# Moving the low halves of the x blocks from VectorE to GpSimd, each ahead of the tap products two steps later

## The chip, the cores and the metric

The kernel runs on one core of a Trainium2 chip. The metric is the time of one execution on the device in microseconds (us); less is better. The core has TensorE (PE, matmuls; its weight loads are listed apart as PEld), VectorE (DVE), ScalarE (ACT), GpSimd (POOL) and the queue engine SyncE (SP), which only issues transfers here.

## The reference, cut to what matters

```python
# x: (4, 512, 16, 32), float32
x = x + conv_mix(ln_c(x), w3, w7, w15, w_mix)      # causal depthwise convs of 3, 7, 15 taps, then a 96 -> 32 mix
t = to_tokens(x)                                    # 2048 tokens of 512
t = t + moe(ln_t(t), gate_w, w1, w2, w3)            # 8 experts, top 2: (silu(t w1) * (t w3)) w2
```

## The kernel before, in words

Every float32 product is made on TensorE as three products of a high and a low half: a = hi + lo, where hi is the value rounded to the type that TensorE takes at full rate (float32r) and lo = a - hi. So each tile that TensorE reads needs two further instructions: a copy that makes hi (ScalarE), and a subtraction that makes lo.

The program has three stages. The first is the convolution, written as matmuls: for each output block, the filter taps times the mixing matrix (the "tap products", a 128 x 512 to 128 x 1280 matrix `wc`) are the weights, and a normalised block of x, shifted, is what streams. The second routes the tokens, the third runs the experts. The change touches the first alone.

The first stage runs in 26 steps t. Steps 0 to 14 are five output blocks of three steps each (4, 4 and 6 tiles of 128 columns of `wc`, so 512, 512 and 768 columns); steps 15 to 25 are one output block each. While steps 0 to 14 run, the 16 blocks of x are still being prepared, one a step. There is no scheduler: each engine's list is written out by hand, and semaphores (counters that one engine raises and another waits for) tie them together. For step t these instructions are what the text below speaks of:

- DVE, iteration t: `x_join(t+1)` (four BATCH_NORM_AGGREGATE from PSUM, L1117), `x_stats(t+2)` (four BATCH_NORM_STATS2, L1108, and `spread`, a TENSOR_TENSOR of 96 elements, L1111), `x_scales(t+1)` (RECIPROCAL, L1122, and `nb`, a SCALAR_TENSOR_TENSOR of 4 elements, L1123), `wc_low(t)` (the low half of the tap products, L1149), `x_low(t)` (the low half of block t of x, L1143), and after steps 2, 5, 8, 11 `add_conv` (L1154), which takes a finished output block out of PSUM.
- ACT, iteration t: `x_deviation(t+1)` (a square root, L597), `x_normal(t+1)` (four ACTIVATE that write the normalised block `xs`, L604, and one that writes its high half, L609), `wc_high(t+2)` (L592).
- POOL: `multiply_taps(t)`, the tap products of step t (L442, in one to four instructions), which waits for `wc_low(t-3)`, since `wc` has three buffers. For t from 3 on these are POOL's only work in this stage.
- PE, iteration t: `x_moments(t+2)` (L791; x_join needs its result, and it needs `spread`), then `conv(t)` (L823 to L825), which waits for `x_low(t)` and `wc_low(t)`.
- SP: `join_halves`, transfers that copy parts of two finished x blocks side by side for the last product of an output block. They wait for `x_low` of those blocks.

`xs` has two buffers, so `x_normal(t+1)` also waits for `x_low(t-1)`.

Of the kernel before, what the change touches and what calls it, by code (L numbers as in the profile page):

```python
# [8 lines left out]
ALU = mybir.AluOpType  # L9
# [8 lines left out]
NBLK = 16  # L18
# [4 lines left out]
PAD = max(LAGS) // NQ - 1  # L23
WB = 3
# [49 lines left out]
def ended(t):  # L74
    return [p for p in range(NBLK) if last_step(p) == t]
# [20 lines left out]
def chunks(t):  # L96

    h = NBLK - 1 - (t // NS if t < NS * LONG else t - 2 * LONG)
    two = pair(h)
    single = [p for p in head_parts(h) if p not in two]  # L100
    each = two + tuple(single)
    runs = [(n, blk, j, LAGS[n] // NQ - (1 if (n, blk, j) in two else 0)) for n, blk, j in each]
    if t < NS * LONG:
        runs = [runs[t % NS]]
    if t >= NS * LONG or t % NS == NS - 1:
        runs.append((two[0][0], None, 1 if two[0][2] == 1 else 0, 1))
    return runs
# [24 lines left out]
def metaformer(nc, xt, taps_d, mix_d, joint_d, gate_d, units, out):  # L132

    with ExitStack() as ctx:
        def at(name, byte, shape, dt=F32):

            with ExitStack() as s:
                if byte:
                    s.enter_context(nc.sbuf_tensor(f"under_{name}", [P, byte // 4], F32))
                return s.enter_context(nc.sbuf_tensor(name, shape, dt))  # L140

        def sem(name):
            return ctx.enter_context(nc.semaphore(name))
# [7 lines left out]
        xs_hi, xs_lo = xs_parts[:, :, 0, :, :], xs_parts[:, :, 1, :, :]  # L151
# [5 lines left out]
        xs = [at(f"xs{n}", small_at + 2944 + 2 * KB * n, [P, NB, P]) for n in range(2)]  # L157
# [103 lines left out]
        pads = sem("pads")  # L261
        x_spread, x_hop, x_var, x_sd, x_scale = (sem("x_spread"), sem("x_hop"), sem("x_var"), sem("x_sd"),
                                                 sem("x_scale"))
        x_norm, x_hi_out, x_lo_out = sem("x_norm"), sem("x_hi_out"), sem("x_lo_out")
# [64 lines left out]
        def _(sp):  # L329
# [12 lines left out]
            def join_halves(p):  # L342

                blocks = [NBLK - 1 - blk for _, blk, _ in pair(NBLK - 1 - p)]
                last = LAGS[pair(NBLK - 1 - p)[0][0]] // NQ - 1
                sp.wait_ge(x_lo_out, max(blocks) + 1)
                if p >= ZB:
                    sp.wait_ge(step_ps, last_step(p - ZB) + 1)
                for m, r in enumerate(blocks):
                    for half in range(2):  # L350
                        rows = slice(2 * D * m + D * half, 2 * D * m + D * half + D)
                        sp.dma_start(joint[p % ZB][rows].bitcast(F32),
                                     xs_parts[2 + half::NQ, r, :, :, PAD - last:PAD - last + P].bitcast(F32)
                                     ).then_inc(joint_st[p % ZB], 16)
# [51 lines left out]
        def _(pool):  # L406
# [22 lines left out]
            def multiply_taps(t):  # L429

                if t >= WB:
                    pool.wait_ge(wc_lo_out, t - WB + 1)
                at_col = 0
                head = NBLK - 1 - (t // NS if t < NS * LONG else t - 2 * LONG)
                for n, blk, j, count in chunks(t):
                    first, shape = TAP_AT[n] + LAGS[n] * (blk or 0), [P, count, D, NQ]
                    lags, mixing = taps[:, first:first + count * NQ], mixT[:, j, :]
                    if blk is None:
                        pool.wait_ge(joint_in, 16)
                        lags = joint_w[:, NQ * head:NQ * head + NQ]  # L440
                        mixing = joint_w[:, NBLK * NQ + D * j:NBLK * NQ + D * j + D]
                    ins = pool.tensor_tensor(  # L442
                        wc[t % WB][:, at_col:at_col + count * P].rearrange("p (a d q) -> p a d q", d=D, q=NQ),
                        lags.rearrange("p (a q) -> p a q", q=NQ).unsqueeze(2).broadcast_to(shape),
                        mixing.unsqueeze(1).unsqueeze(3).broadcast_to(shape), ALU.mult)
                    at_col += count * P
                ins.then_inc(wc_ready, 1)
# [21 lines left out]
            pool.iota(tokid[:], pattern=[[P, NT]], base=1, channel_multiplier=1, **flat).then_inc(consts, 1)  # L469

            pool.wait_ge(taps_in[1], 16)
            for t in range(WB, STEPS):
                multiply_taps(t)

            def gather(buffer, index, landed):
# [310 lines left out]
        def _(pe):  # L786
# [14 lines left out]
            def conv(t, between):  # L801

                pe.wait_ge(x_lo_out, min(t + 1, NBLK))
                pe.wait_ge(wc_lo_out, t + 1)
                p = t // NS if t < NS * LONG else t - 2 * LONG
                opens, closes = t >= NS * LONG or t % NS == 0, last_step(p) == t
                if opens and p >= 2:
                    pe.wait_ge(resid, p - 1)
                out_bank = B[p % 2][:].rearrange("p (b i) -> p b i", i=P)
                at_col = 0  # L810
                runs = chunks(t)
                for m, (n, blk, _, count) in enumerate(runs):
                    if m == 1 and t >= NS * LONG:
                        between()
                    if blk is None:
                        pe.wait_ge(joint_st[p % ZB], 64 * (p // ZB + 1))
                    for a in range(count):
                        cols, at_x = slice(at_col, at_col + P), slice(PAD - a, PAD - a + P)
                        hi, lo = ((joint[p % ZB][:, 0, :, :], joint[p % ZB][:, 1, :, :]) if blk is None else
                                  (xs_hi[:, NBLK - 1 - blk, :, at_x], xs_lo[:, NBLK - 1 - blk, :, at_x]))  # L820
                        first = opens and m == 0 and a == 0
                        final = closes and m == len(runs) - 1 and a == count - 1
                        pe.matmul(out_bank, wc_hi[t % WB][:, cols], hi, start=first, stop=False)  # L823
                        pe.matmul(out_bank, wc_hi[t % WB][:, cols], lo, start=False, stop=False)  # L824
                        ins = pe.matmul(out_bank, wc_lo[t % WB][:, cols], hi, start=False, stop=final)  # L825
                        at_col += P
                ins.then_inc(step_ps, 1)
# [268 lines left out]
        def _(dve):  # L1096
# [29 lines left out]
            def x_stats(r):  # L1126
                dve.wait_ge(x_in[r], 16)
                if r >= 2:
                    dve.wait_ge(x_hop, r - 1)
                spread_moments(XT[r], r % 2).then_inc(x_spread, 1)  # L1130

            def x_join(r):
                dve.wait_ge(x_hop, r + 1)
                join_moments(6 + r % 2, 4 + r % 2).then_inc(x_var, 1)

            def x_scales(r):
                dve.wait_ge(x_sd, r + 1)
                scale_of(4 + r % 2).then_inc(x_scale, 1)

            def x_low(r):  # L1140
                dve.wait_ge(x_hi_out, r + 1)
                dve.wait_ge(pads, 2)
                dve.tensor_tensor(xs_lo[:, r, :, PAD:], xs[r % 2][:], xs_hi[:, r, :, PAD:], ALU.subtract).then_inc(x_lo_out, 1)  # L1143

            def wc_low(t):

                cols = slice(0, columns(t))
                dve.wait_ge(wc_hi_out, t + 1)
                dve.tensor_tensor(wc_lo[t % WB][:, cols], wc[t % WB][:, cols], wc_hi[t % WB][:, cols],  # L1149
                                  ALU.subtract).then_inc(wc_lo_out, 1)  # L1150

            def add_conv(p):
                dve.wait_ge(step_ps, last_step(p) + 1)
                ins = dve.tensor_tensor(XT[p][:], B[p % 2][:].rearrange("p (b i) -> p b i", i=P), XT[p][:], ALU.add)  # L1154
                ins.then_inc(resid, 1)
# [94 lines left out]
            for t in range(NS * LONG):  # L1250
                x_join(t + 1)
                if t + 2 < NBLK:
                    x_stats(t + 2)
                x_scales(t + 1)
                wc_low(t)
                x_low(t)
                for p in ended(t - 2):
                    if p < LONG - 1:
                        add_conv(p)
            x_low(NBLK - 1)  # L1260
            wc_low(NS * LONG)
            dve.wait_ge(consts, CONSTS)
            then_next(dve.tensor_tensor(upto_e[:], rank8[:].unsqueeze(1).broadcast_to([P, E, E]),
# [208 lines left out]
```

## Time and profile before

| | us |
|---|---|
| median of 3 runs | 774.92 (774.66 to 775.23) |
| profiled execution, its own time | 776.01 |
| its span, first to last instruction | 774.3 |
| PE busy | 725.0 (94%) |
| DVE busy | 353.6 (46%) |
| ACT busy | 321.2 (41%) |
| POOL busy | 198.2 (26%) |

The profile is one execution, recorded by the hardware. The shares are means over three stages with different limits: PE is 94% busy overall, and its pauses sit at the start, in the stretch up to 76 us, and around the routing at 147 to 200 us. So the first stage has to be read by itself, from its own rows.

### The profile page before, as it was taken

How to read it: one execution, taken by the hardware profiler on the slowest of the kernel's cores; microseconds unless marked ns; L12 is line 12 of the kernel's file. 1: busy time of each engine (PE TensorE's matmuls, PEld its weight loads, DVE VectorE, ACT ScalarE, POOL GpSimd, SP SyncE). 2: the span in 40 equal slices, each digit the busy share in tenths (PEclk: the TensorE clock that was granted, in tenths of full speed). 3: DMA queues.
4: the chain of work that ended last, by engine and by line, in shares of the span. 5: the costliest groups of instructions: out<-in, count | busy, mean ns of one | idle time of the engine just before them, and what ended most of it. 6: DMA issues, size and time to landing. Idle time of an engine off the chain costs nothing.

```text
span 774.3 us, 9557 instructions
## 1 busy us (share of the span) xinstructions
PE 725.0 (94%) x3544; PEld 588.5 (76%) x3545; DVE 353.6 (46%) x749; ACT 321.2 (41%) x504; POOL 198.2 (26%) x208
## 2 busy tenths in 40 slices
PE   3998999855999999999999999999999999999994
PEld 2776888743778778877888887778888888888883
DVE  5887756785336225531543452245325334532410
ACT  6777555543135415333434442344435234443310
POOL 5337311003601240124011502510252224021011
PEclk9999999955999999999999999999999999999998
DMA  7336777662243653074318414721653274152013
GB/s 243 66 60 112 149 169 157 158 233 68 70 193 125 188 139 113 14 217 110 112 29 257 113 55 105 236 72 54 201 126 113 41 245 122 59 151 28 3 14 42
DMA packets 55970, 92.20 MB, mean 119 GB/s; under 512 B 7536, under 2 KB 40688, under 8 KB 49776
## 3 DMA queue, kind: packets, MB, share of 16 engines
q1 hardware_dynamic: 45728, 71.64, 30.3%
q0 software_dynamic: 9472, 19.43, 12.8%
q8 instruction: 32, 0.52, 0.3%
q10 hardware_dynamic: 720, 0.46, 0.2%
q14 instruction: 18, 0.15, 0.1%
HBM read 65.49 MB, written 17.63 MB: 107 GB/s over the span
## 4 chain that ended last, share of the span: by engine, by line
PE 85%; DVE 7%; DMA 2%; issue 2%; ACT 2%; POOL 1%; SPq 0%; POOLq 0%; ACTq 0%; DVEq 0%
PE bank L920 22%; PE bank L922 22%; PE bank L921 22%; PE bank L823 3%; PE bank L824 3%; PE bank L825 3%; PE bank L915 2%; PE bank L990 2%; PE bank L845 1%; DVE bn L1108 1%; DVE wc_lo L1149 1%; PE bank L1012 1%; PE bank L863 1%; DVE mv L1117 1%; PE bank L838 1%
## 5 line engine op out<-in xcount | busy, mean ns | idle before, releaser
L920 PE MATMUL bank<-xT_hi,w_hi 128*128 128x512 f32 x495 | 194.1, 392 | 1.5 <-DVE xT_lo L1323 1.5
L922 PE MATMUL bank<-xT_hi,w_lo 128*128 128x512 f32 x495 | 193.8, 392 | 0.0
L921 PE MATMUL bank<-xT_lo,w_hi 128*128 128x512 f32 x495 | 193.8, 392 | 0.0
L496 POOL DMA_INDIRECT out_x<-y,dst_i x40 | 62.1, 1553 | 265.1 <-ACT y L690 130.4
L1330 DVE TENSOR_TENSOR h<-bank,h 128x512 f32<-128x512 f32 x64 | 44.2, 691 | 175.9 <-PE bank L922 175.9
L321 DVE TENSOR_TENSOR w_lo<-w_raw,w_hi 128x2048 fp32r<-128x2048 f32 x48 | 109.7, 2288 | 17.6 <-ACT w_hi L316 17.5
L920 PEld LDWEIGHTS bank<-xT_hi,w_hi 128*128 128x128 f32 x495 | 93.6, 189 | 21.4 <-DVE xT_lo L1323 1.8
L922 PEld LDWEIGHTS bank<-xT_hi,w_lo 128*128 128x128 f32 x495 | 93.5, 189 | 19.6
L921 PEld LDWEIGHTS bank<-xT_lo,w_hi 128*128 128x128 f32 x495 | 93.6, 189 | 19.5
L920 PE MATMUL bank<-w_hi,hT_hi 128*128 128x512 f32 x249 | 99.2, 398 | 0.0
L922 PE MATMUL bank<-w_hi,hT_lo 128*128 128x512 f32 x249 | 97.3, 391 | 0.0
L921 PE MATMUL bank<-w_lo,hT_hi 128*128 128x512 f32 x249 | 97.0, 389 | 0.0
L316 ACT ACTIVATE w_hi<-w_raw 128x2048 fp32r<-128x2048 f32 x48 | 91.8, 1912 | 7.0 <-DMA w_raw<-in_units 7.0
L675 ACT ACTIVATE hT_hi<-h 128x512 fp32r<-128x512 f32 x64 | 40.4, 632 | 120.3 <-DVE h L1330 120.3
L477 POOL DMA_INDIRECT xg<-xn_rows,src_i x32 | 33.2, 1039 | 203.3 <-PE bank L915 143.8
L669 ACT ACTIVATE h<-bank 128x512 f32<-128x512 f32 x64 | 38.3, 598 | 110.0 <-PE bank L922 110.0
L690 ACT ACTIVATE y<-bank,gate_row 128x512 f32<-128x512 f32 x32 | 22.0, 688 | 126.9 <-PE bank L922 126.9
L1323 DVE TENSOR_TENSOR xT_lo<-bank,xT_hi 128x512 fp32r<-128x512 f32 x32 | 22.1, 690 | 95.3 <-ACT xT_hi L661 95.3
L1334 DVE TENSOR_TENSOR hT_lo<-h,hT_hi 128x512 fp32r<-128x512 f32 x64 | 44.4, 693 | 44.6 <-ACT hT_hi L675 44.6
L823 PE MATMUL bank<-xs_parts,wc_hi 128*128 128x512 f32 x128 | 54.9, 429 | 6.5 <-DVE xs_parts L1143 6.5
L442 POOL TENSOR_TENSOR wc<-taps,mixT 128x256 f32<-128x256 f32 (+4 forms) x48 | 41.7, 887 | 74.1 <-DVE wc_lo L1149 71.4
L922 PEld LDWEIGHTS bank<-w_hi,hT_lo 128*128 128x128 f32 x249 | 46.7, 188 | 10.2
(166 smaller groups left out, 885.7 us busy)
## 6 DMA issues: line engine op xcount, KB each, us to landing
w_raw<-in_units SPq DMA_DIRECT2D x48, 1024.0 KB, 5.2
joint<-xs_parts SPq DMA_DIRECT2D x64, 128.0 KB, 3.8
out_x<-XT SPq DMA_DIRECT2D x17, 256.0 KB, 3.5
XT<-in_x SPq DMA_DIRECT2D x16, 256.0 KB, 6.8
xn_rows<-xnb SPq DMA_DIRECT2D x16, 256.0 KB, 2.5
gate_row<-gate_rows,gate_i POOLq DMA_INDIRECT x40, 2.8
out_x<-y,dst_i POOLq DMA_INDIRECT x40, 4.8
xg<-xn_rows,src_i POOLq DMA_INDIRECT x32, 4.0
```

The source lines that it names most:

```text
L316: eng.activation(w_hi[k][:], raw[:], ACT.Copy).then_inc(hi_ready[k], 1)
L321: eng.tensor_tensor(w_lo[k][:], raw_of(e, k)[0][:], w_hi[k][:], ALU.subtract).then_inc(lo_ready[k], 1)
L442: ins = pool.tensor_tensor(wc[t % WB][:, at_col:at_col + count * P].rearrange("p (a d q) -> p a d q", d=D, q=NQ), lags.rearrange("p (a q) ...
L496: pool.indirect_dma_start(out=out, out_offset=bass.IndirectOffsetOnAxis(ap=index, axis=0), in_=rows, in_offset=None, compute_op=ALU.add).t ...
L669: act.activation(h[m % 2][:], B[2 * (m % 2)][:], ACT.Silu).then_inc(silu_out, 1)
L675: act.activation(hT_hi[:, m, :], h[m % 2][:], ACT.Copy).then_inc(hT_hi_out, 1)
L823: pe.matmul(out_bank, wc_hi[t % WB][:, cols], hi, start=first, stop=False)
L920: pe.matmul(bank, stationary[0], moving[0], start=start, stop=False)
L921: pe.matmul(bank, stationary[0], moving[1], start=False, stop=False)
L922: return pe.matmul(bank, stationary[1], moving[0], start=False, stop=stop)
L1330: dve.tensor_tensor(h[m % 2][:], B[2 * (m % 2) + 1][:], h[m % 2][:], ALU.mult).then_inc(h_out, 1)
L1334: dve.tensor_tensor(hT_lo[:, m, :], h[m % 2][:], hT_hi[:, m, :], ALU.subtract).then_inc(hT_lo_out, 1)
```

## The change

`x_low` goes from DVE's list to POOL's. It computes the same subtraction from the same tiles into the same place. On POOL, `x_low(0)` stands ahead of the loop over the tap products, and `x_low(t-2)` ahead of `multiply_taps(t)` for t = 3 to 17. The `pads` wait falls away, since POOL writes the pads itself.

```diff
@@ gpsimd
             pool.wait_ge(taps_in[1], 16)
+
+            def x_low(r):
+                pool.wait_ge(x_hi_out, r + 1)
+                pool.tensor_tensor(xs_lo[:, r, :, PAD:], xs[r % 2][:], xs_hi[:, r, :, PAD:], ALU.subtract).then_inc(x_lo_out, 1)
+
+            x_low(0)
             for t in range(WB, STEPS):
+                if t - WB + 1 < NBLK:
+                    x_low(t - WB + 1)
                 multiply_taps(t)
@@ vector
-            def x_low(r):
-                dve.wait_ge(x_hi_out, r + 1)
-                dve.wait_ge(pads, 2)
-                dve.tensor_tensor(xs_lo[:, r, :, PAD:], xs[r % 2][:], xs_hi[:, r, :, PAD:], ALU.subtract).then_inc(x_lo_out, 1)
-
@@
                 wc_low(t)
-                x_low(t)
                 for p in ended(t - 2):
                     if p < LONG - 1:
                         add_conv(p)
-            x_low(NBLK - 1)
             wc_low(NS * LONG)
```

Where it stands on the engines: first POOL, before, from the end of its constants (`tokid`) into the loop, steps 3 to 5 and on. `wc` is the tap products, `wc_lo_out` the count of finished `wc_low`.

```order
29 L469 IOTA tokid 128x16
30 L442 TENSOR_TENSOR wc<-taps,mixT 128x512 [waits wc_lo_out,taps_in1]
31 L442 TENSOR_TENSOR wc<-taps,mixT 128x512 [waits wc_lo_out]
32 L442 TENSOR_TENSOR wc<-taps,mixT 128x640 [waits wc_lo_out]
33 L442 TENSOR_TENSOR wc<-joint_w 128x128 [waits joint_in]
```

POOL at the same place after the change; L475 is `x_low`, and `x_hi_out` counts the high halves that ACT has written.

```order
29 L469 IOTA tokid 128x16
30 L475 TENSOR_TENSOR xs_parts<-xs,xs_parts 128x4x128 [waits x_hi_out,taps_in1]
31 L475 TENSOR_TENSOR xs_parts<-xs,xs_parts 128x4x128 [waits x_hi_out]
32 L442 TENSOR_TENSOR wc<-taps,mixT 128x512 [waits wc_lo_out]
33 L475 TENSOR_TENSOR xs_parts<-xs,xs_parts 128x4x128 [waits x_hi_out]
34 L442 TENSOR_TENSOR wc<-taps,mixT 128x512 [waits wc_lo_out]
35 L475 TENSOR_TENSOR xs_parts<-xs,xs_parts 128x4x128 [waits x_hi_out]
36 L442 TENSOR_TENSOR wc<-taps,mixT 128x640 [waits wc_lo_out]
37 L442 TENSOR_TENSOR wc<-joint_w 128x128 [waits joint_in]
```

The tap products of a step now also stand behind ACT's high half of a block of x, and a subtraction and a product follow each other.

DVE before, its iteration for step 2 (768 columns), and the first instruction of the next.

```order
37 L1111 TENSOR_TENSOR spread<-bn_0,maskq 128x96 [waits dve_step]
38 L1122 RECIPROCAL rs<-rs 128x4 [waits x_sd]
39 L1123 SCALAR_TENSOR_TENSOR nb<-mv,rs 128x4 [waits dve_step]
40 L1149 TENSOR_TENSOR wc_lo<-wc,wc_hi 128x768 [waits wc_hi_out]
41 L1143 TENSOR_TENSOR xs_parts<-xs,xs_parts 128x4x128 [waits pads,x_hi_out]
42 L1117 BN_AGGR mv<-bank 128x2 [waits x_hop]
```

DVE after, the same place; the lines of the file have moved, the instructions are the same ones.

```order
35 L1119 TENSOR_TENSOR spread<-bn_0,maskq 128x96 [waits dve_step]
36 L1130 RECIPROCAL rs<-rs 128x4 [waits x_sd]
37 L1131 SCALAR_TENSOR_TENSOR nb<-mv,rs 128x4 [waits dve_step]
38 L1152 TENSOR_TENSOR wc_lo<-wc,wc_hi 128x768 [waits wc_hi_out]
39 L1125 BN_AGGR mv<-bank 128x2 [waits x_hop]
```

One instruction has gone from each iteration, the one between `wc_low` and the next `x_join`.

## Rows read from the trace of the kernel before

**Rows 1.** Windows: busy us (instructions) of each engine, granted clock, DMA share, GB/s
```profile
14.00:76.00 62.00, 57.64 (x238) 45.35 (x239) 49.52 (x187) 46.78 (x103) 30.17 (x30) 1.00 0.41 76
76.00:147.00 71.00, 71.00 (x401) 60.59 (x401) 49.90 (x206) 38.28 (x88) 14.35 (x31) 1.00 0.79 166
```

**Rows 2.** Waits from 12 to 80 us: engine, releaser, total us, times, longest
```profile
PE bank L823 <- DVE xs_parts L1143: 6.5, 10, 2.3
```

**Rows 3.** Timeline of DVE, steps 7 and 8: start, us, instruction, [idle before]
```profile
40.01 0.63 DVE L1117 BATCH_NORM_AGGREGATE mv<-bank 128x2 f32<-128x24 f32 x4 [1.55 <-PE bank L791]
40.56 0.81 DVE L1108 BATCH_NORM_STATS2 bn<-XT 128x6 f32<-128x128 f32 x4
41.41 0.26 DVE L1111 TENSOR_TENSOR spread<-bn,maskq 128x96 f32<-128x96 f32 x1
...
41.79 0.16 DVE L1123 SCALAR_TENSOR_TENSOR nb<-mv,rs 128x4 f32<-128x4 f32 x1
...
42.47 0.68 DVE L1143 TENSOR_TENSOR xs_parts<-xs,xs_parts 128x512 fp32r<-128x512 f32 x1
43.07 0.68 DVE L1154 TENSOR_TENSOR XT<-bank,XT 128x512 f32<-128x512 f32 x1
...
45.52 0.95 DVE L1149 TENSOR_TENSOR wc_lo<-wc,wc_hi 128x768 fp32r<-128x768 f32 x1
46.38 0.69 DVE L1143 TENSOR_TENSOR xs_parts<-xs,xs_parts 128x512 fp32r<-128x512 f32 x1
...
51.88 0.63 DVE L1117 BATCH_NORM_AGGREGATE mv<-bank 128x2 f32<-128x24 f32 x4 [1.61 <-PE bank L791]
```

**Rows 4.** Timeline of PE: the first matmuls of steps 8 and 14
```profile
47.13 0.51 PE L823 MATMUL bank<-xs_parts,wc_hi 128*128 128x512 f32 x1 [0.62 <-DVE xs_parts L1143]
...
71.25 0.50 PE L823 MATMUL bank<-xs_parts,wc_hi 128*128 128x512 f32 x1 [1.26 <-DVE xs_parts L1143]
```

**Rows 5.** Timeline, all engines: high half of block 0 and the start of step 0
```profile
11.10 0.63 ACT L609 ACTIVATE xs_parts<-xs 128x512 fp32r<-128x512 f32 x1
...
12.77 0.69 DVE L1149 TENSOR_TENSOR wc_lo<-wc,wc_hi 128x512 fp32r<-128x512 f32 x1
...
13.37 0.68 DVE L1143 TENSOR_TENSOR xs_parts<-xs,xs_parts 128x512 fp32r<-128x512 f32 x1
...
14.11 0.79 PE L823 MATMUL bank<-xs_parts,wc_hi 128*128 128x512 f32 x1 [2.30 <-DVE xs_parts L1143]
```

**Rows 6.** Timeline of POOL: an affine select and two tap products
```profile
1.83 0.52 POOL L423 TENSOR_SCALAR_AFFINE_SELECT sumq<-ones 128x128 f32<-128x128 f32 x1
...
5.60 1.05 POOL L442 TENSOR_TENSOR wc<-taps,mixT 128x512 f32<-128x512 f32 x1 [2.66 <-DMA mixT<-in_mix]
...
24.49 0.40 POOL L442 TENSOR_TENSOR wc<-joint_w 128x128 f32<-128x128 f32 x1
```

**Rows 7.** Timeline, all engines: POOL and DVE where both have work
```profile
72.11 0.69 DVE L1143 TENSOR_TENSOR xs_parts<-xs,xs_parts 128x512 fp32r<-128x512 f32 x1 [0.91 <-ACT xs_parts L609]
...
72.21 1.28 POOL L442 TENSOR_TENSOR wc<-taps,mixT 128x384 f32<-128x384 f32 x1
...
72.72 2.12 DVE L1149 TENSOR_TENSOR wc_lo<-wc,wc_hi 128x1280 fp32r<-128x1280 f32 x1
...
73.45 1.64 POOL L442 TENSOR_TENSOR wc<-joint_w 128x128 f32<-128x128 f32 x1
```

**Rows 8.** Timeline, all engines: two small DVE instructions beside tap products
```profile
7.11 2.26 POOL L442 TENSOR_TENSOR wc<-taps,mixT 128x512 f32<-128x512 f32 x2
...
9.16 0.23 DVE L1123 SCALAR_TENSOR_TENSOR nb<-mv,rs 128x4 f32<-128x4 f32 x1
...
24.71 0.29 DVE L1111 TENSOR_TENSOR spread<-bn,maskq 128x96 f32<-128x96 f32 x1
```

**Rows 9.** Timeline of ACT: block 8 of x, normalised, and its high half
```profile
41.98 1.65 ACT L604 ACTIVATE xs<-XT,nb,rs 128x128 f32<-128x128 f32 x4 [1.00 <-DVE nb L1123]
43.67 0.63 ACT L609 ACTIVATE xs_parts<-xs 128x512 fp32r<-128x512 f32 x1
```

## The prediction

> **What bounds the kernel now.** I read the windows first, since the shares of the whole span mix three stages. From 76 to 147 us PE is busy for 71.00 us of 71.00 [rows 1]: whatever PE gains or loses before 76 us is passed on unchanged. From 14 to 76 us, the steps 0 to 14 that the change touches, it is busy for 57.64 of 62.00 us, so at most 4.4 us lie there, and a little before 14 us. The granted clock is full (1.00) in both windows, with pauses such as the 1.26 us before 71.25 [rows 4] in them, so I charge nothing for the clock. The table of waits says what PE waits for: ten times, 6.5 us in all, for the low half of x [rows 2], 2.3 us of it ahead of its first matmul [rows 5]; 4.2 us are left for the other nine.
>
> The timeline of DVE shows why [rows 3]. In every three steps there is one stretch in which DVE works without a gap from the join of the moments at 40.01 to the low half at 46.38, through two iterations and an `add_conv`; 0.06 us after the end of that low half PE starts step 8 at 47.13 [rows 4]. The next such stretch begins at 51.88, when PE is through step 8 and the next moments. So the loop is 7.12 us on DVE and 4.75 us on PE, 11.87 us for three steps. Two `x_low` lie in the first part.
>
> **What the change removes.** An `x_low` occupies DVE for 0.60 us (from 42.47 to 43.07) [rows 3]. The first of the two leaves the loop with 0.60; the second leaves it with 0.61, because PE then waits for `wc_low` (0.95 from 45.52, so 46.47) and not for 46.38 + 0.69 = 47.07. That is 1.21 us off each three steps. At the start, step 0 waits for `wc_low` (12.77 + 0.69 = 13.46) in place of 14.05 [rows 5]: 0.6 us off. `x_low(0)` on POOL does not stand in the way: its input is there at 11.73 [rows 5].
>
> **What it costs on POOL.** The trace of before shows no GpSimd subtraction of two full tiles. The nearest row is the tap product of the same 512 elements, 1.05 us with nothing beside it; the other end is an affine select, 0.52 us for 128 elements, 2.1 us for 512 [rows 6]. The product has two inputs and one output like the subtraction, but its inputs are repeated small ones, so I take 1.10 us, near that row, and keep 1.05 and 2.1 as ends. POOL has the time: per step 1.10 and 1.05 (or 1.27 + 0.40 for the six-tile steps, 1.27 being 1.05 and another 128 elements by the slope of (1.05 - 0.40)/3 = 0.22) in about 4 us, and the low half is ready well before PE asks for it.
>
> **What it costs on DVE: turns at the memory.** This decides the sign. At 72.11 DVE reads two tiles of SBUF. POOL's product of 384 elements, which begins at 72.21, would take 0.84 by the slope and takes 1.28: it ends at 73.49 as if it had begun at 72.65, when DVE had read its 512 elements. DVE's next subtraction, of 1280 elements from 72.72, would take 1.49 (0.69 for 512 and 0.95 for 768 make 0.26 for each 256 more) and takes 2.12: it is held until 73.35, 0.14 before POOL's end. And POOL's product of 128 elements, 0.40 alone, then takes 1.64 [rows 7]: it had to let the waiting DVE go first. So an instruction of one of the two that reads two SBUF tiles excludes such a one of the other for its whole length, and who waits gets the next turn. DVE's small ones obey it too: `nb` took 0.23 for 0.16 at 9.16, until 0.14 before the end (9.37) of two tap products, and `spread` 0.29 for 0.26 at 24.71, until 0.14 before the end (24.89) of one [rows 8]. Instructions with one SBUF input (the moments, the reciprocal, `add_conv`) are not held: `add_conv` at 43.07 took its 0.68 beside a tap product [rows 3].
>
> The Trainium skill has this as a rule ("SBUF — State Buffer", Who interferes with whom): a DVE instruction with two SBUF inputs contends with a GpSimd instruction that reads SBUF, and the later one blocks fully; the trace agrees, with the 2.12 us. Its page "GPSIMD Engine Reference" (3.1) has 4497 ns for a two-input add of 2048 elements, so an estimate of 1.1 to 1.2 us for ours; the sum below would be the same within 0.4 us.
>
> Before the change POOL reads for one product a step, set off by the end of `wc_low`, while DVE goes on to `x_low` and then to the moments: hardly ever is DVE the one that waits. Now `x_low(t)` and `multiply_taps(t+2)` stand back to back, 2.1 us, set off by ACT's high half. I walk the loop with this, 0 being the join at 40.01, POOL's lock lasting until 0.14 before its end:
>
> - `x_low(7)` starts at about 0.2, 0.05 after ACT's high half of block 7, and `multiply_taps(9)` behind it holds the memory from 1.2 to 2.1. `spread` arrives at 1.4 and waits until 2.1: **0.75 lost**.
> - `nb` goes out at 2.5, and 0.2 later ACT starts block 8: 1.69 to its high half, and 0.63 for it [rows 9]. So `x_low(8)` starts at 5.1. DVE meanwhile does `wc_low(7)`, `add_conv`, the next moments (join 0.55, statistics 0.85) and comes to `spread` at 5.2: it waits until 6.06, **0.86 lost**.
> - `multiply_taps(10)` is at the memory until 7.1; `nb` comes at 6.45: **0.65 lost**. Then `wc_low(8)`, and PE starts step 8 at 8.2 where it was 7.12.
>
> The third iteration loses next to nothing: DVE waits there for ACT or PE anyway. So 2.26 lost against 1.21 won: +1.05 us for three steps.
>
> **The sum.** Start: -0.5 (0.6, less a little for `wc_low(0)` waiting for POOL). Three full loops, steps 2 to 11: +3.2. The last, steps 11 to 14: the four pieces of `multiply_taps(15)` are short, DVE gets in after some 0.3 and 0.2, and step 14 now waits for `wc_low(14)`; of the 1.05 I leave 0.4. Together +3.1 us, and PE is full afterwards, so this is the kernel's. On the profiled execution, 776.01 us (span 774.3), it makes 779.1; that one ran 1.1 us above the median of 774.92, to which the same sum gives **778.0**. With 1.05 or 1.2 us for `x_low` the same walk gives +2.4 to +3.5. SP's transfers of the joined halves wait for `x_low` of two blocks and are used at the end of a step, several us later; they hide.
>
> **The rivals.** The measurement tells 0.2% (1.55 us) from no change.
>
> 1. *The turns cost DVE little, and the kernel is faster.* If `spread` and `nb` slip in between POOL's two instructions, or POOL's requests come a little later than I have them, the 1.21 per loop is won. PE then keeps only the part of its waits that ACT sets, about 0.5 of the 1.26 before step 14: -0.6 at the start and -3.5 of the 4.2, so -4.1 us, 771. It decides where less than 1.2 us per loop is lost. For it: the two locks on `nb` and `spread` seen so far cost 0.07 and 0.03, so their full length is my extension from the 1280-element row. Against it: their ends agree with the same 0.14.
> 2. *Only part is lost*, say `spread` or `nb` and not both: about 1.2 against 1.2, 774 to 776, no difference.
> 3. *GpSimd's subtraction is much slower*, as a select is. Each 0.1 us more is met by `spread` in nearly every step, 0.25 us a loop and 1.2 over five loops. At 1.5 us this is +6, at 2.1 us about +15: 781 to 790. For it: another output type (fp32r) than any GpSimd row writes; against: the product's row.
> 4. *The subtraction on POOL delays the tap products* and through `wc_high` the next step. It has 3.5 us from one high half to the next and needs 2.2 to 2.8, so this alone costs nothing at 1.10, and joins rival 3 above 1.7 us.
>
> **How the numbers follow.** My forecast 0.52 (776.5 to 780.5 by itself), rival 1 0.22, rival 2 0.12, rival 3 with 4 0.14. Faster by over 0.2%: 0.22; same 0.13, with a little of the forecast's lower edge; slower 0.65. The range takes in rival 1 and the lower half of rival 3: 770.5 to 784.
>
> **What would show it.** In the new trace: `x_low` on POOL at 1.1 us when alone; `spread` and `nb` with durations of 0.8 to 1.1 us instead of 0.26 and 0.16, two or three times in three steps; PE's waits ascribed to `wc_low`, some 1.4 us before steps 5, 8 and 11, in place of 0.62; from 76 us on nothing changed but the shift. Step 0 starts near 13.6. I am wrong if `spread` keeps its 0.26 beside POOL's work (rival 1), or if `x_low` shows 1.5 us or more outside any overlap (rival 3).

## The result, and the profile after

The changed kernel takes **782.3 us** (median of 5 runs, 781.28 to 783.01) against 774.92 (774.06 to 775.85) of the kernel before: a ratio of 1.0089, 95% interval 1.0078 to 1.0100. It is slower, by 7.4 us where 3.1 were forecast. Timed a second time, on another occasion, it took 781.2 us (4 runs, 780.3 to 782.63) against 775.1: 1.0077, 1.0060 to 1.0094. The two profiled executions are closer together than the medians, 781.28 against 776.01 us (spans 779.3 and 774.3), since that of before lay 1.1 us above its median and that of after 1.0 below. The accounts below are of these two.

The head of the page of after, busy time of each engine and its share of the span:

```profile
PE 725.2 (93%) x3544; PEld 588.2 (75%) x3545; DVE 355.0 (46%) x733; ACT 320.4 (41%) x504; POOL 220.3 (28%) x224
```

The windows of after, the counterpart of [rows 1], with the columns named there; the windows of 2 us lie around step 14:

```profile
14.00:76.00 62.00, 52.79 (x220) 40.85 (x221) 48.13 (x166) 44.80 (x101) 41.09 (x38) 0.99 0.40 71
74.00:76.00 2.00, 0.62 (x2) 0.56 (x3) 2.00 (x2) 1.97 (x5) 2.00 (x3) 0.82 1.23 218
76.00:78.00 2.00, 2.00 (x6) 1.62 (x5) 1.97 (x3) 0.71 (x2) 2.00 (x2) 0.50 1.20 158
78.00:80.00 2.00, 2.00 (x8) 1.56 (x7) 0.81 (x2) 0.62 (x1) 2.00 (x4) 0.83 1.18 233
81.00:152.00 71.00, 71.00 (x403) 60.80 (x402) 49.56 (x204) 38.33 (x88) 15.32 (x33) 1.00 0.72 154
```

From 14 to 76 us PE is busy for 52.79 us instead of 57.64, and POOL for 41.09 instead of 30.17. DVE has 21 instructions fewer in that window but only 1.39 us less busy time (48.13 against 49.52): what it saved in subtractions it spends inside other instructions. After 81 us PE is full again at a full clock, so the loss is made before; only some 0.8 us of it comes back later. And from 76 to 78 us the granted clock is 0.50, half, which has no counterpart in the kernel before.

The table of waits of after, 12 to 85 us, and POOL and DVE in the groups of the first 80 us (count, busy us, mean ns, idle before):

```profile
PE bank L831 <- DVE wc_lo L1152: 11.0, 9, 2.2
```

```profile
L475 POOL TENSOR_TENSOR xs_parts<-xs,xs_parts 128x512 fp32r<-128x512 f32 x16 | 20.6, 1288 | 22.3 <-ACT xs_parts L617 22.3
L1131 DVE SCALAR_TENSOR_TENSOR nb<-mv,rs 128x4 f32<-128x4 f32 x16 | 8.8, 551 | 0.5
L1119 DVE TENSOR_TENSOR spread<-bn,maskq 128x96 f32<-128x96 f32 x16 | 8.6, 536 | 0.5
```

PE's waits for the low half of x [rows 2] are gone, and 11.0 us of waits for `wc_low` stand in their place. GpSimd's subtraction takes 1.29 us each of 16 times. `nb`, which works on 4 elements a partition, takes 551 ns on average and `spread` 536.

One loop of three steps of after, from the timeline of all engines (the counterpart of [rows 3]):

```profile
40.25 0.63 ACT L617 ACTIVATE xs_parts<-xs 128x512 fp32r<-128x512 f32 x1
...
40.48 0.63 DVE L1125 BATCH_NORM_AGGREGATE mv<-bank 128x2 f32<-128x24 f32 x4 [1.35 <-PE bank L799]
...
40.96 1.29 POOL L475 TENSOR_TENSOR xs_parts<-xs,xs_parts 128x512 fp32r<-128x512 f32 x1 [0.35 <-ACT xs_parts L617]
...
41.87 0.50 DVE L1119 TENSOR_TENSOR spread<-bn,maskq 128x96 f32<-128x96 f32 x1
...
42.21 1.07 POOL L442 TENSOR_TENSOR wc<-taps,mixT 128x512 f32<-128x512 f32 x1
...
42.49 0.81 DVE L1131 SCALAR_TENSOR_TENSOR nb<-mv,rs 128x4 f32<-128x4 f32 x1
...
43.82 0.68 DVE L1157 TENSOR_TENSOR XT<-bank,XT 128x512 f32<-128x512 f32 x1
44.05 0.47 PE L831 MATMUL bank<-xs_parts,wc_hi 128*128 128x512 f32 x1 [0.55 <-DVE wc_lo L1152]
...
45.72 1.29 POOL L475 TENSOR_TENSOR xs_parts<-xs,xs_parts 128x512 fp32r<-128x512 f32 x1 [2.44 <-ACT xs_parts L617]
45.80 1.32 DVE L1119 TENSOR_TENSOR spread<-bn,maskq 128x96 f32<-128x96 f32 x1
...
46.96 1.07 POOL L442 TENSOR_TENSOR wc<-taps,mixT 128x512 f32<-128x512 f32 x1
47.24 0.80 DVE L1131 SCALAR_TENSOR_TENSOR nb<-mv,rs 128x4 f32<-128x4 f32 x1
...
47.97 0.95 DVE L1152 TENSOR_TENSOR wc_lo<-wc,wc_hi 128x768 fp32r<-128x768 f32 x1
...
49.06 0.47 PE L831 MATMUL bank<-xs_parts,wc_hi 128*128 128x512 f32 x1 [1.42 <-DVE wc_lo L1152]
```

Read each DVE row beside the POOL row above it. `spread` of 45.80 goes out 0.08 us after GpSimd's subtraction (45.72 to 47.01) and ends at 47.12; `nb` of 47.24 ends at 48.04, with the product (46.96 to 48.03). `add_conv` at 43.82, which has one input in PSUM, took its 0.68. Against the 0.26 and 0.16 of [rows 3] the two lose 0.24, 0.65, 1.06 and 0.64: 2.59 us in this loop, against 1.21 won by the subtractions removed. Their ends follow from the 0.14 us that the prediction read off [rows 8]: 47.01 - 0.14 + 0.26 is 47.13 for `spread`, 48.03 - 0.14 + 0.16 is 48.05 for `nb`. The loop is 13.29 us long (joins at 40.48 and 53.77) instead of 11.87: 8.58 on DVE, until 49.06, and 4.71 on PE. By PE's waits it comes to nearly the same: 1.42 us in place of 0.62 before the third step of the loop, and a new wait of 0.55 before its second (44.05), 1.35 more in all.

The starts of steps by PE's timeline, before and after:

| step | before | after | difference | gained since the row above |
|---|---|---|---|---|
| 0 | 14.11 | 13.81 | -0.30 | -0.30 |
| 2 | 23.46 | 22.57 | -0.89 | -0.59 |
| 11 | 58.99 | 62.31 | +3.32 | +4.21 |
| 14 | 71.25 | 75.38 | +4.13 | +0.81 |
| 15 | 75.35 | 81.19 | +5.84 | +1.71 |

The last row is the clock. PE's timeline of after, around step 14:

```profile
75.38 0.77 PE L831 MATMUL bank<-xs_parts,wc_hi 128*128 128x512 f32 x1 [2.21 <-DVE wc_lo L1152]
...
76.80 0.63 PE L831 MATMUL bank<-xs_parts,wc_hi 128*128 128x512 f32 x1
...
78.83 0.40 PE L833 MATMUL bank<-xs_parts,wc_lo 128*128 128x512 f32 x1
...
81.19 0.40 PE L831 MATMUL bank<-xs_parts,wc_hi 128*128 128x512 f32 x1
```

PE waits for 2.21 us, then works through some three microseconds in which one matmul takes 0.63 us and not 0.40; the granted clock there is 0.50, which is the lower of the two levels, 1.2 GHz instead of 2.4. Step 14 is 5.81 us long instead of 4.10.

What ends that wait stands in the same stretch of the timeline of all engines:

```profile
71.99 1.29 POOL L475 TENSOR_TENSOR xs_parts<-xs,xs_parts 128x512 fp32r<-128x512 f32 x1
72.06 1.27 ACT L600 ACTIVATE wc_hi<-wc 128x1280 fp32r<-128x1280 f32 x1 [0.34 <-POOL wc L442]
...
73.23 0.28 ACT L605 ACTIVATE rs<-mv,eps 128x4 f32<-128x4 f32 x1
73.23 2.69 POOL L442 TENSOR_TENSOR wc<-taps,mixT 128x256 f32<-128x256 f32 x3
73.55 0.18 DVE L1130 RECIPROCAL rs<-rs 128x4 f32<-128x4 f32 x1 [2.44 <-ACT rs L605]
73.76 0.16 DVE L1131 SCALAR_TENSOR_TENSOR nb<-mv,rs 128x4 f32<-128x4 f32 x1
73.84 3.43 DVE L1152 TENSOR_TENSOR wc_lo<-wc,wc_hi 128x768 fp32r<-128x768 f32 x2
```

Here the queue is another one: ACT's high half of 1280 elements (72.06) waits for POOL's products, `rs` of the next block stands behind it on ACT, DVE idles for 2.44 us waiting for `rs`, and only then comes the `wc_low` that PE wants. The last row is two instructions. The first, of 768 elements, is the one that step 14 needs; by itself it takes 1.40 us where 0.95 is its time alone, so 0.45 us of the wait are a turn lost by DVE beside POOL's products, and the rest came about ahead of it.

### The profile page after: what moved, and what is told of

It reads as the page before. It is cut to its first block, busy times and chain, and to the rows that moved or that the text cites. A ratio compares the mean times of both kernels' runs of the same rounds, so it can differ in the third digit from the quotient of the medians.

```text
span 779.3 us, 9541 instructions
## 1 busy us (share of the span) xinstructions
PE 725.2 (93%) x3544; PEld 588.2 (75%) x3545; DVE 355.0 (46%) x733; ACT 320.4 (41%) x504; POOL 220.3 (28%) x224
## 3 DMA queue, kind: packets, MB, share of 16 engines
q0 software_dynamic: 9472, 19.43, 12.7%
## 4 chain that ended last, share of the span: by engine, by line
PE 83%; DVE 7%; DMA 3%; issue 2%; ACT 2%; POOL 1%; SPq 0%; POOLq 0%; ACTq 0%; DVEq 0%
PE bank L928 21%; PE bank L930 21%; PE bank L929 21%; PE bank L831 3%; PE bank L832 2%; PE bank L833 2%; PE bank L998 2%; PE bank L923 2%; PE bank L853 1%; DMA out_x<-y,dst_i 1%; DVE bn L1116 1%; PE bank L1020 1%; DVE wc_lo L1152 1%; PE bank L871 1%; DVE spread L1119 1%
## 5 line engine op out<-in xcount | busy, mean ns | idle before, releaser
L504 POOL DMA_INDIRECT out_x<-y,dst_i x40 | 64.2, 1606 | 261.8 <-ACT y L698 126.6
L929 PEld LDWEIGHTS bank<-w_lo,hT_hi 128*128 128x128 f32 x249 | 46.8, 188 | 9.2
```

The costliest lines, as they stand in the source:

```text
L504: pool.indirect_dma_start(out=out, out_offset=bass.IndirectOffsetOnAxis(ap=index, axis=0), in_=rows, in_offset=None, compute_op=ALU.add).t ...
L929: pe.matmul(bank, stationary[0], moving[1], start=False, stop=False)
```

## The experiments

The theory under test, **A**: a DVE instruction with two SBUF inputs and a GpSimd instruction that reads SBUF take turns for their whole length, and what `spread`, `nb` and `wc_low` lose by this is the whole loss of the loops. The rivals: **B**, PE waits for data that come later because the GpSimd subtraction is slow, whatever DVE's small ones do; **C**, the subtraction pushes POOL's tap products, and with them `wc_high`, back. The clock fall was an open matter of its own.

**The inputs moved to PSUM.** In the changed kernel one of the two inputs of `spread` (its mask) and of `nb` (mean and variance) comes from free columns of PSUM banks; nothing else moves.

```
+        for k in range(2):
+            mv[4 + k] = B[5][:, 448 + 8 * k:456 + 8 * k].rearrange("p (b s) -> p b s", s=2)
+        mask_ps = B[3][:, 480:484]
...
-              maskq[:].unsqueeze(1).unsqueeze(3).broadcast_to(shape), ALU.mult)
+              (mask_ps if slot < 2 else maskq[:]).unsqueeze(1).unsqueeze(3).broadcast_to(shape), ALU.mult)
...
+            then_next(dve.tensor_copy(mask_ps, maskq[:]))
```

> The changed kernel, but each of VectorE's two small instructions of an iteration, spread and nb, has one of its two inputs in PSUM instead of SBUF (the mask in bank 3, the moments of the x blocks in bank 5). GpSimd's order and work stay as in the changed kernel. Theory (turns at SBUF between instructions with two SBUF inputs): the small two are no longer held, spread keeps 0.26 us and nb 0.16 to 0.22; three steps take some 11.2 us instead of 13.25; step 15 starts about 2.8 us earlier than in the kernel before the change, the kernel takes about 772 us. Rival (the loss is that the tap products now stand behind ScalarE's high half and the slow subtraction): nothing changes against the changed kernel, 781 to 782 us, and VectorE waits instead for wc_hi.

Measured: 772.38 us (6 runs, 771.44 to 773.14) against 775.28, ratio 0.9962 (0.9950 to 0.9975): 10 us below the changed kernel, and faster than the kernel before, about the 772 expected. Its timeline of all engines, at the same place of a loop:

```profile
38.39 1.30 POOL L480 TENSOR_TENSOR xs_parts<-xs,xs_parts 128x512 fp32r<-128x512 f32 x1
...
39.64 1.06 POOL L447 TENSOR_TENSOR wc<-taps,mixT 128x512 f32<-128x512 f32 x1
...
39.81 0.26 DVE L1124 TENSOR_TENSOR spread<-bn,bank 128x96 f32<-128x96 f32 x1
...
40.19 0.16 DVE L1136 SCALAR_TENSOR_TENSOR nb<-bank,rs 128x4 f32<-128x4 f32 x1
40.27 0.98 DVE L1157 TENSOR_TENSOR wc_lo<-wc,wc_hi 128x512 fp32r<-128x512 f32 x1
```

GpSimd's two instructions stand there as before, 1.30 and 1.06 us, and `spread` and `nb` beside the product take 0.26 and 0.16. `wc_low`, which still has two SBUF inputs, comes next and takes 0.98 instead of 0.68, since it is held until the product is over; the next one, of 768 elements (43.70), takes 1.19 instead of 0.95. So a part of the hold has moved to `wc_low`, 0.54 us in this loop, and that is most of why the loop gains some 0.5 us on the kernel before and not the full 1.21. The loops are 11.3 us, and the waits before steps 5, 8 and 11 are 0.22 to 0.45. B and C fall as explanations of the loops: GpSimd's work is unchanged and the loss is gone.

**The products first.** The order on POOL turned round: the tap products three steps on, then the subtraction.

```
             for t in range(WB, STEPS):
+                multiply_taps(t)
                 if t - WB + 1 < NBLK:
                     x_low(t - WB + 1)
-                multiply_taps(t)
```

> The changed kernel with the two GpSimd calls of a step in the other order: the tap products of step t first, then the low half of block t-2. The products are then set free by wc_low of three steps earlier as in the kernel before, and only the subtraction runs just behind ScalarE's high half. Theory (turns): nb is mostly free, spread is still held by up to 1.1 us in every third step; about +0.7 us against the kernel before, 775 to 776.5 us. Rival (a slower subtraction late for TensorE): the low half is later than in the changed kernel, so no better than 781 us, and TensorE waits for GpSimd's low half.

Measured: 776.15 us (10 runs, 775.11 to 777.15), ratio 1.0009 (0.9999 to 1.0018), in the expected range. The loops are 12.09 us, PE's waits in them 0.78. The same instructions in another order cost 6 us less; `spread` has a mean of 622 ns (more than the 536 of the changed kernel) and `nb` of 352 (less than 551). Over 16 blocks the two are 1.8 us shorter together, less than a third of what the order gained. So the sum of the held time doesn't decide by itself; that it matters whether a hold falls into the stretch in which DVE works without a gap is the likely reason, and wasn't tested apart.

**The subtraction on both engines.** The kernel before, with its own subtraction on DVE, and the same one again on GpSimd into a spare tile that nobody reads.

```
+            def x_again(r):
+                pool.wait_ge(x_hi_out, r + 1)
+                if r:
+                    pool.wait_ge(x_again_out, r)
+                pool.tensor_tensor(scratch[:], xs[r % 2][:], xs_hi[:, r, :, PAD:], ALU.subtract).then_inc(x_again_out, 1)
...
+                    act.wait_ge(x_again_out, r - 1)
```

> The kernel before, with the subtraction of the low half done on both engines: VectorE's as before and used, and the same again on GpSimd at the places of the change, into a spare tile that nobody reads (ScalarE waits for it as well before it overwrites xs). This is the cost of the change without its gain. Theory (turns): each subtraction on VectorE and each spread and nb can be held too; three steps take some 14.3 us instead of 11.81, step 15 starts about 11 us later than in the kernel before, the kernel takes 785 to 788 us. Rival (GpSimd's work is free beside VectorE's): 775 us, with the ends of VectorE's instructions unchanged.

Measured: 789.48 us (4 runs, 788.97 to 790.33), ratio 1.0187 (1.0170 to 1.0204). The loop without a clock fall in it is 14.50 us (steps 8 to 11, 53.45 to 67.95), with a wait of 1.72 us ahead of it and behind; `spread` takes 827 ns on average, `nb` 729, DVE's own subtraction 741. This is the cost without the gain: 2.63 us a loop, where 2.59 were added up above. That the two are so close is partly chance, since `spread` and `nb` are held longer here than in the changed kernel and DVE's own subtraction is held too. It came out 1.5 us above the upper end expected; the granted clock fell twice in its profile, from 38 to 44 and from 82 to 88 us, which the expectation didn't count. The loop with the first fall in it is 14.84 us long, 0.3 more than the next.

**A fill in place of the subtraction.** GpSimd writes the same tile at the same place but reads nothing; the low half of x is left out of the products by this.

```
-  pool.tensor_tensor(xs_lo[:, r, :, PAD:], xs[r % 2][:], xs_hi[:, r, :, PAD:], ALU.subtract).then_inc(x_lo_out, 1)
+  pool.memset(xs_lo[:, r, :, PAD:].bitcast(F32), 0.0).then_inc(x_lo_out, 1)
```

> The changed kernel, but GpSimd fills the low half of each x block with zeros in place of the subtraction, at the same place and after the same wait: it writes the same tile and reads none. The low half of x is left out of the computation. Theory (turns, of reads): the fill takes 0.6 us and holds nobody, the tap products behind it start 0.7 us earlier and still read; +0.9 us against the kernel before, about 776 us, with nb or spread held by the tap products alone. Rival (GpSimd's writes hold VectorE as well, or the order itself costs): spread is held by the fill too, and the time stays at 779 us or more.

Measured: 775.92 us (10 runs, 775.22 to 776.64), ratio 1.0008 (0.9998 to 1.0018), as expected. Its timeline of all engines shows both kinds of neighbour:

```profile
44.51 0.53 POOL L475 MEMSET xs_parts<- 128x512 f32 x1 [2.80 <-ACT xs_parts L617]
44.60 0.26 DVE L1119 TENSOR_TENSOR spread<-bn,maskq 128x96 f32<-128x96 f32 x1
...
44.99 1.05 POOL L442 TENSOR_TENSOR wc<-taps,mixT 128x512 f32<-128x512 f32 x1
...
45.40 0.65 DVE L1131 SCALAR_TENSOR_TENSOR nb<-mv,rs 128x4 f32<-128x4 f32 x1
```

`spread` lies inside the 0.53 us of the fill and takes 0.26; `nb`, 0.8 us later, lies inside the product, which reads, and takes 0.65, until 46.05 where the product ends at 46.04. The hold needs GpSimd to read. The Trainium skill states it so ("SBUF — State Buffer", Who interferes with whom: not with one that only writes), and the trace agrees. The kernel isn't as fast as the one with the inputs in PSUM; the likely reason is that the product, 0.8 us earlier now, still holds both in other places (`spread` and `nb` have means of 464 and 467 ns in the first 80 us).

**One input at a time.** Only `nb`'s, then only `spread`'s, by the same lines as above.

> The changed kernel with one input of nb alone in PSUM; spread keeps its two SBUF inputs. Theory (turns): nb is at 0.16 us, spread is still held, and since GpSimd's chain behind ScalarE stays, part of what nb no longer waits is waited elsewhere; the walk with 1.29 us for the subtraction gives +1.8 us against the kernel before at step 15, so 776.5 to 777.5 us if TensorE's clock stays up before step 14. Rival (only spread costs): as the changed kernel, 781 us or more.

> The changed kernel with one input of spread alone in PSUM; nb keeps its two SBUF inputs. Theory (turns): spread at 0.26 us, nb held by up to 1.1 us; the walk gives +0.4 us against the kernel before at step 15, so 775 to 776 us. Rival (only nb costs): as the changed kernel, 781 us or more.

Measured: `nb` alone 777.79 us (7 runs, 776.76 to 779.79), ratio 1.0039 (1.0027 to 1.0051); `spread` alone 778.46 (5 runs, 776.66 to 778.62), 1.0030 (1.0016 to 1.0044). The loops are 12.35 and 12.21 us, the waits in them 1.11 and 0.74. Each takes 0.9 to 1.1 us off a loop of 13.29, and both together 2.0 (to 11.3), so the two losses add up. Which of the two costs more isn't told apart: by the medians it is `nb`'s kernel that is faster, by the ratios `spread`'s. The first is 0.3 us above the 777.5 at the upper end of what was expected. The second came out 2.5 us above the 775 to 776 expected: its profile has a clock fall from 72 to 78 us, which `nb` alone doesn't show, but step 14 had already begun 1.06 us later than in the kernel before (72.31), where the whole forecast was +0.4 at step 15.

**The last three blocks back on DVE.** The low half of blocks 13 to 15 made on DVE again, so that POOL comes to the products of the last steps without them. This was to tell whether the wait of 2.21 us before step 14 is what brings the clock down.

```
+LATE = 13
...
-                if t - WB + 1 < NBLK:
+                if t - WB + 1 < LATE:
                     x_low(t - WB + 1)
...
+                if t >= LATE:
+                    x_low(t)
...
+            x_low(NBLK - 1)
```

> The changed kernel, but the low halves of the last three blocks, 13 to 15, are made by VectorE again, at their old places. Steps 0 to 12 are as in the changed kernel. This looks at the last loop, where TensorE waited 2.2 us before step 14 and its granted clock then fell to half until 78.5 us. Theory (the long wait is what GpSimd's queue makes: low half 14 and the four-piece tap products stand ahead of what wc_low(14) needs, and the fall of the clock comes with it): the wait before step 14 is near the 1.26 us of before, the clock stays at full, step 14 starts some 3.5 us later than in the kernel before (71.25) and step 15 no later than that; 1.5 to 2 us less than the changed kernel, 779.5 to 780.5. Rival (the fall of the clock has nothing to do with the wait): it falls here as well and the time stays at 781 us or more.

Measured: 780.17 us (4 runs, 778.87 to 781.51), ratio 1.0055 (1.0038 to 1.0072): the median is in the expected range, the profiled execution, 781.51, is not. The wait before step 14 is 1.29 us, and there the clock stays full. But it falls elsewhere, right after the first of the 1.42 us waits; its windows:

```profile
34.00:36.00 2.00, 0.60 (x3) 0.30 (x2) 1.97 (x5) 0.90 (x3) 1.05 (x2) 1.00 0.50 110
36.00:38.00 2.00, 1.92 (x5) 1.56 (x6) 1.46 (x9) 1.97 (x5) 0.52 (x1) 0.57 0.00 0
38.00:40.00 2.00, 2.00 (x6) 1.56 (x6) 1.20 (x3) 1.30 (x5) 2.00 (x2) 0.58 0.02 4
```

and again from 62 to 68. The loop behind the first fall is 13.93 us long (36.08 to 50.01), the next 13.24: 0.7 us lost here. In the profile of the changed kernel that same wait, before steps 5, 8 and 11, passed three times without a fall. A fall inside the loops costs less than the 1.71 us at step 14, since a part of PE's slower work takes the place of its next wait. With two falls in it, this execution reached step 14 at 77.03, 5.8 us later than the kernel before, and not 3.5. So the median met the forecast by luck as far as this profile tells: the wait before step 14 did shrink as expected, and the thought behind the experiment, that the fall belongs to step 14, is not borne out.

**The subtraction in two halves.** Two GpSimd instructions of 256 elements in place of one of 512: more work on GpSimd, but DVE can get in between.

```
-  pool.tensor_tensor(xs_lo[:, r, :, PAD:], xs[r % 2][:], xs_hi[:, r, :, PAD:], ALU.subtract).then_inc(x_lo_out, 1)
+  for b in (0, NB // 2):
+      two = slice(b, b + NB // 2)
+      ins = pool.tensor_tensor(xs_lo[:, r, two, PAD:], xs[r % 2][:, two], xs_hi[:, r, two, PAD:], ALU.subtract)
+  ins.then_inc(x_lo_out, 1)
```

> The changed kernel with GpSimd's subtraction in two instructions of 256 elements each in place of one of 512. It costs GpSimd about 0.15 us more a block. Theory (a GpSimd instruction with SBUF inputs keeps VectorE's two-input one out for its whole length, and who waits gets the next turn): spread slips in between the two halves and waits 0.6 us at most instead of 1.1, and the kernel gains in spite of more work on GpSimd: +2.1 us at step 15 against the kernel before, in place of +3.9, so 777 to 779.5 us. Rival (it is the sum of GpSimd's work that counts): 782 us or more.

Measured: 778.98 us (5 runs, 777.54 to 780.64), ratio 1.0046 (1.0032 to 1.0060), in the expected range. From its timeline of all engines:

```profile
44.96 1.45 POOL L477 TENSOR_TENSOR xs_parts<-xs,xs_parts 128x256 fp32r<-128x256 f32 x2 [2.44 <-ACT xs_parts L620]
45.04 0.77 DVE L1122 TENSOR_TENSOR spread<-bn,maskq 128x96 f32<-128x96 f32 x1
```

The two halves take 1.45 us where the whole took 1.29, and `spread`, which again goes out 0.08 us after GpSimd, is through after 0.77 us and not 1.32: it waits for one instruction and not for both. Loops 12.7 us instead of 13.25. The hold is by instruction, and the waiting one gets the next turn.

**The PSUM inputs without the change.** The lines of the first experiment put into the kernel before.

> The kernel before (low half of x on VectorE) with one input of spread and of nb in PSUM, as in e1_small_psum. It tells whether what e1_small_psum gains over the kernel before is the move of the subtraction or the PSUM inputs alone. Theory (turns): in the kernel before spread and nb are hardly ever held, so nothing changes, 774.5 to 775.5 us; the gain of 2.9 us in e1_small_psum is the move's. Rival (PSUM inputs are what gains): 772 to 773 us.

Measured: 775.58 us (10 runs, 774.76 to 776.09), ratio 1.0005 (0.9995 to 1.0014). That is the upper end of what was expected (775.5). By themselves the PSUM inputs are worth nothing; the 0.4% of the first experiment is what the move of the subtraction is worth once it no longer holds `spread` and `nb`.

**Both remedies.** The first experiment with the last three blocks back on DVE.

> e1_small_psum with the low halves of the last three blocks, 13 to 15, back on VectorE, for the best version. Theory (turns): the low halves of blocks 0 to 12 are free on GpSimd, and the last three no longer stand ahead of the four-piece tap products of steps 15 to 17, for which ScalarE waited 1.42 and 2.48 us in e1_small_psum while TensorE still had work; -2.8 us at step 15 against the kernel before in both, so 772 us, the same as e1_small_psum within 0.5 us. Rival (the tail of e1_small_psum costs): 771 us or less.

Measured: 772.57 us (5 runs, 771.96 to 772.86), ratio 0.9965 (0.9951 to 0.9978), the same as without them. The first experiment remains the best version, 0.38% faster than the kernel before.

**Both kernels once more.**

> The changed kernel once more, for a second profile. The difference of the medians, 7.4 us, is larger than that of the two profiles, 5.0 us. Theory (TensorE's granted clock falls to half for 3 to 4 us in some executions, at different steps, where the kernel has pauses of 1.4 us or more, each fall costing 1.7 us): one or two such falls between 14 and 90 us, not necessarily at step 14; three steps take 13.25 us where the clock is full; median 781 to 783 us. Rival (the fall belongs to the 2.2 us wait before step 14): exactly one, at the same place.

> The kernel before once more, for a second profile. Theory: its pauses of 0.2 to 1.3 us leave the granted clock at full from 20 to 147 us, as in the first profile. Rival (the clock falls in any kernel in some executions): a fall there too.

Measured: the changed kernel 781.2 us as given above, span of its profile 779.7; the kernel before 775.23 in one run, span 773.5. The changed kernel's loops are 13.25 us again (steps 5, 8 and 11 at 36.20, 49.45 and 62.69), and its clock fell at the same place again, from 76 to 80 us; the kernel before kept its clock from 14 to 150 us in both profiles. One fall, at the same place, is what the rival had said, and not the theory, which had one or two at different steps; the median was in the theory's range. For the changed kernel the place repeated in its two profiles, though the kernel with the last three blocks on DVE shows that a fall isn't tied to that step.

## Why the prediction was right in sign and short in size

**The number.** 782.3 us is slower, as forecast, but by more than twice the 3.1 us. It lies outside the 776.5 to 780.5 that the forecast had for itself, and inside 770.5 to 784 only because that range took in part of rival 3, a much slower subtraction, which isn't what happened.

**The bound and the mechanism: right.** PE was full after 76 us and is full after 81, and the loss lies ahead of that. The step on which the sign hung, "an instruction of one of the two that reads two SBUF tiles excludes such a one of the other for its whole length, and who waits gets the next turn", was worked out from one place [rows 7] and is borne out by `spread` at 1.32 us, by the PSUM inputs, by the fill and by the halves. One word of it is too narrow: the kernels tell only that GpSimd must read, not that it needs two tiles.

**"I take 1.10 us" for the subtraction: too low.** It takes 1.29, 0.24 above the product row on which the estimate rested [rows 6] and far below the 2.1 of the select. The estimate of 1.1 to 1.2 from the Trainium skill's "GPSIMD Engine Reference" (3.1) was low as well. This moved the places of the losses: `spread` meets the end of the subtraction and not the product, and `nb` meets the product.

**The loop: +1.42 us and not +1.05.** Of the four holds the three that were named (0.75, 0.86, 0.65) came out as 0.24, 1.06 and 0.64, and a fourth, `nb` of the first iteration, 0.65, was missing: 2.59 instead of 2.26. The rest of the difference is 0.04 in the two parts of the loop. "With 1.05 or 1.2 us for `x_low` the same walk gives +2.4 to +3.5" had already said that a longer `x_low` costs more; three loops made +4.21 where +3.2 was put. "Some 1.4 us before steps 5, 8 and 11" came out at 1.42, which is partly luck: the holds behind it came out otherwise, and the new wait of 0.55 us in the middle of the loop wasn't forecast.

**The start: more than "-0.5".** Step 0 began at 13.81 (13.6 was named) but by step 2 the lead was 0.89.

**The last loop: +0.81 and not +0.4.** That `wc_low` would be what PE waits for was right, but the prediction looked for the loss in DVE's turns. The row before the `wc_low` of 73.84 shows a chain through ACT as well: the high half behind POOL's products, `rs` behind the high half, DVE idle for 2.44 us. That is rival 4, thought harmless at 1.10 us, and in this one place it is not. Taking three subtractions out of this stretch shortened the wait before step 14 from 2.21 to 1.29 us; of the 2.21, 0.45 are the turn that the `wc_low` itself lost (1.40 for 0.95); how much of the rest is the chain and how much turns lost before it was not told apart.

**"I charge nothing for the clock": the step that failed.** The reason given was that pauses such as 1.26 us [rows 4] leave it full. The pause before step 14 grew to 2.21 us and the clock went to half for some 3 us, which cost 1.71 us, the largest single miss. The rows of before couldn't show what a longer pause does; what they did show is that 1.26 was safe, and the prediction itself had PE waiting for longer than that, "some 1.4 us".

**The account.** The span is 5.0 us longer where 3.1 were forecast: start -0.4 against the forecast, loops +1.0, last loop +0.4, clock +1.7, and 0.8 given back after step 15 (the token indices that the routing makes for the gather are 5.3 us later than before, 184.1 against 178.8, the end 5.0). The median is 7.4 longer; 2.1 of the other 2.4 us are what the two profiled executions differ from their medians (1.1 and 1.0), the rest that spans and times differ. Executions of the changed kernel aren't alike, and the mean granted clock on record for each goes with it: 0.963 to 0.965 in the five of the first timing (781.28 to 783.01 us); in the second 0.965 and 0.962 in two (781.75 and 782.63), and 0.967, like the kernel before, in the other two, which took 780.3 and 780.64. So it's likely that some executions pass without a fall of the clock, at a cost of 5.2 to 5.5 us over 775.1, and that others lose more to it than the profiled ones. The mean also holds the low clock around the routing, so this is a sign and not a count; only two executions have a profile.

**The rivals.** Rival 1 fell with `spread` at 1.32 us, rival 2 with `spread` and `nb` both held, 2.59 us a loop. Rival 3 needed 1.5 us or more. Its price for a slower subtraction, 1.2 us for each 0.1, would have made 2.3 of the 0.19 us; the loops and the last one together came out 1.4 above the forecast, so the price was too high if anything.

**What stays open.** What makes the clock fall. It fell in both profiles of the changed kernel, in that with the subtraction on both engines (twice), with `spread`'s input in PSUM, and with the last three blocks back (twice), each time behind a wait of PE of 1.4 us or more. It didn't in those whose waits behind step 0, up to 90 us, were at most 1.29 us: both of before, its version with PSUM inputs, the two with all PSUM inputs and the change, and the fill. But waits of 1.46 us (products first), 2.21 (`nb`'s input in PSUM) and 2.35 (two halves) passed without one too, and so did those of 1.8 to 2.6 us ahead of step 0 in all of them. A long wait goes with it and doesn't decide it.

## What to carry to other kernels

Before moving an elementwise operation from DVE to GpSimd, look for what DVE then does beside it: each DVE instruction with two SBUF inputs, however small, can be held for a whole GpSimd instruction that reads, so count the instructions that can be caught and not their busy time. If the caught ones are small, give them one input in PSUM; that turned a move that cost 0.9% into one that gains 0.4%. And where a change lengthens a pause of PE beyond any that the profile shows, put the price of one clock fall, 0.3 to 1.7 us here, into the range at least.

## What the runs showed of the hardware

- A DVE operation of 4 elements a partition took up to 0.81 us, five times its 0.16, beside a GpSimd product of 1.07 us.
- A GpSimd fill of 512 elements (0.53 us) held nothing, where a GpSimd instruction that reads did.
- The hold works the other way too: GpSimd's tap product of 384 elements took 1.28 us beside DVE's subtraction, 0.84 by the slope [rows 7]. With that subtraction gone from DVE, its products of 512 elements fell from 1345 to 1111 ns on average over the first 80 us, while those of 640 rose from 1518 to 1610.
- GpSimd subtracts 512 elements a partition in 1.29 us and 256 in 0.74 (mean of 32, some of them held); products with repeated small inputs take 1.05 for the same 512.
